# Four 1024-column additions on GpSimd become eight of 512 columns, each placed behind a VectorE split; the FFN sums get a buffer of their own

## The chip, the core and the metric

The kernel runs on one core of one Trainium2 chip. The metric is the device time of one execution in microseconds (us). A profiled execution leaves a trace: for every engine each instruction with its start and its duration. TensorE (PE) multiplies matrices, VectorE (DVE), ScalarE (ACT) and GpSimd (POOL) work element by element, SyncE (SP) issues transfers. The engines run apart from one another and meet at semaphores: an instruction waits until a counter has reached a value, and adds to one when it is done.

## What is computed

The input x has 2 x 2048 tokens of 256 values. After a layer norm, two branches work on the normed value xn, and both are added to x.

```
xn = layernorm(x)
h  = xn + cosformer_attn(rmsnorm(xn, norm1_w), qkv_w, qkv_b, out_w, out_b)
m  = gelu(rmsnorm(h, norm2_w) @ mlp_w1 + mlp_b1) @ mlp_w2 + mlp_b2
f  = relu(xn @ ternary(w_fc).T + gate * low_rank(xn)) ** 2 @ ternary(w_proj).T
out = x + (h + m) + f
```

The attention is causal and linear: q and k go through a relu, are weighted with cosines and sines of the position, and each token sums over those before it.

## The kernel before

Eight tiles (t = 0 to 7) of 512 tokens, 256 of each batch, pass one after the other through a body that is written once per engine. In a body PE goes through these stages: four chunks of attention (j = 0 to 3; scores, the context within and across chunks, and the update of a running `state`), between them the first blocks of the FFN branch, then the output projection, the rest of the FFN, and last eight MLP blocks (m = 0 to 7). In the MLP stage PE takes `mlp_up(m)` and then `mlp_down(m - 1)`; between them it also makes k, q, z and v of the next tile. The order on each engine is that of its code; there is no scheduler.

Matrix products are made in float32 of reduced width, so each operand that matters is held as a high and a low part. The low part of a hidden block comes from VectorE: `split(n)` (L945) subtracts `wide_hi` from `wide`, n = 0 to 7 for the FFN blocks, n = 8 to 15 for the MLP blocks. It waits for ScalarE, which writes `wide` and then `wide_hi` (`hi_done`), and PE's `down(n)` (L1194) waits for it (`lo_done`). Thus each `mlp_down(m)` needs `split(8 + m)`.

GpSimd has four additions of 128 partitions x 1024 columns in a tile, each over all four blocks of 128 tokens:

- L496: `xn` plus the row `ob_row`, right after `trig_q(0)` (L484, two products of 256 columns that weight q of chunk 0; each chunk has such a pair);
- L524: `res = xb + ctxn`, behind `split(7)`; `ctxn` holds h by then, `xb` holds x plus the MLP's second bias;
- L530: `res = res + ctxn`, where VectorE has meanwhile overwritten `ctxn` with the scaled FFN sums (L1033); it waits for `split(9)` and for the split of the next tile's q (`q_parts_done`, the last L795);
- L465: `x_plus_b2`, which refills `xb` for the next tile.

L1033 waits for L524, since both use `ctxn`. At the end VectorE adds the MLP sums to `res` (L1053) and SP sends it out. GpSimd also adds to `state` once per chunk (L510), after VectorE's masked product `mask_update` (L975). `layernorm` (L769) on VectorE makes the next `xn` behind `split(12)`. SP spreads k and q of the next tile by 12 and 24 transfers (`k_stack`, `q_stack`); `trig_q(0)` of that tile waits for the last of them.

Of the kernel before, what the change touches and what calls it, by code (L numbers as in the profile page):

```python
# [84 lines left out]
def program(nc, x, qkv_w, qkv_b, out_w, out_b, norm1_w, norm2_w, mlp_w1, mlp_b1, mlp_w2, mlp_b2,  # L85
            fast_b, w_fc, w_proj, u, v, gate, consts, trig, out):
    with ExitStack() as ctx:
# [268 lines left out]
        @block.sync  # L356
        def _(sp):
            def load_x(t):
                for b in range(B):
                    sp.dma_start(xin[:, 2 * b:2 * b + 2, :],  # L360
                                 x[b, bass.ds(t * POS, POS), :].rearrange("(c p) e -> p c e", p=P)).then_inc(x_in, 16)

            def load_tab(t):
                sp.dma_start(tab[:, :], trig[bass.ds(t, 1), :, :].rearrange("a p n -> p (a n)")).then_inc(tab_in, 16)

            load_x(0)
            sp.dma_start(n1w[:, :], norm1_w.rearrange("(k p) -> p k", p=P),
                         allow_slow_non_contiguous=True).then_inc(in_n1, 16)
            sp.dma_start(raw_qkv, qkv_w.rearrange("(k p) n -> p k n", p=P)).then_inc(in_qkv, 16)
            sp.dma_start(cst[:, :], consts).then_inc(in_const, 16)  # L370
            sp.dma_start(v_raw, v).then_inc(in_fb, 16)
            sp.dma_start(fbT, fast_b.rearrange("r k -> k r"), allow_slow_non_contiguous=True).then_inc(in_fb, 16)
            sp.dma_start(raw_fc, w_fc.rearrange("(m p) n -> p m n", p=P)).then_inc(in_fc, 16)
            sp.dma_start(raw_wo, out_w.rearrange("(k p) n -> p k n", p=P)).then_inc(in_wo, 16)
            smalls = [
                (qkb[:, :], qkv_b[0:2 * E].rearrange("(k p) -> p k", p=P)),
                (n2w[:, :], norm2_w.rearrange("(k p) -> p k", p=P)),
                (u_raw, u.rearrange("(m p) r -> p m r", p=P)),
                (gate_col[:, :], gate.broadcast_to([P, 1])),
                (vb_row[:, :], qkv_b[2 * E:3 * E].rearrange("(a n) -> a n", a=1).broadcast_to([P, E])),  # L380
                (b2_row[:, :], mlp_b2.rearrange("(a n) -> a n", a=1).broadcast_to([P, E])),
                (ob_row[:, :], out_b.rearrange("(a n) -> a n", a=1).broadcast_to([P, E])),
                (b1[:, :], mlp_b1.rearrange("(k p) -> p k", p=P)),
            ]
            assert len(smalls) == N_SMALL
            for dst, src in smalls:
                sp.dma_start(dst, src, allow_slow_non_contiguous=True).then_inc(in_small, 16)
            sp.dma_start(raw_pr, w_proj.rearrange("(m p) n -> p m n", p=P)).then_inc(in_pr, 16)
            load_tab(0)

            sp.wait_ge(shared_full, KE)
            sp.dma_start(raw_w1[0], mlp_w1[0:P, :]).then_inc(in_w1[0], 16)

            def stack(t):

                sp.wait_ge(k_parts_done, (t + 1) * 2 * KE)
                if not isinstance(t, int) or t:
                    sp.wait_ge(shared_full, shared_use(t - 1, S_SCORE + 4 * NB))
                for g in range(4):
                    for slot, part in enumerate((0, 0, 1)):  # L400
                        sp.dma_start(k_stack[slot:P:4, g, :, :].bitcast(F32),
                                     k_parts[32 * g:32 * g + 32, part, :, :]).then_inc(k_stacked, 16)
                sp.wait_ge(q_parts_done, (t + 1) * 2 * KE)
                for g in range(4):
                    stack_q(sp, g, 1, 1, q_lo_stacked)
                for g in range(2 if isinstance(t, int) and t == 0 else 4):
                    for slot in (0, 2):
                        stack_q(sp, g, slot, 0, q_hi_stacked[g // 2])

            sp.wait_ge(stack_zero, 3)  # L410
            stack(0)

            def body(t, more):
                if more:

                    sp.wait_ge(xn_done, (t + 1) * NB)
                    sp.wait_ge(xb_done, t + 1)
                    sp.wait_ge(xs_done, (t + 1) * NB)
                    load_x(t + 1)

                    sp.wait_ge(q_trig_done, (t + 1) * 2 * NB)
                    sp.wait_ge(v_trig_done, (t + 1) * 2 * NB)
                    load_tab(t + 1)
                    stack(t + 1)
                for b in range(B):
                    sp.wait_ge(out_done, t * 2 + b + 1)
                    sp.dma_start(out[b, bass.ds(t * POS, POS), :].rearrange("(c p) e -> p c e", p=P),
                                 res[:, 2 * b:2 * b + 2, :]).then_inc(out_sent, 16)

            body(0, True)  # L430
            with sp.Fori(1, NT - 1) as t:
                body(t, True)
            body(NT - 1, False)
            sp.wait_ge(out_sent, NT * 32)


        @block.gpsimd
        def _(pool):
# [21 lines left out]
                pool.wait_ge(ln_pow, t * N_POW + POW_MSQ)  # L460
                pool.tensor_tensor(msq_eps[:, :], msq[:, :], rms_eps[:, :], ALU.add).then_inc(ln_pow, 1)

            def x_plus_b2(t):

                pool.tensor_tensor(xb[:, :, :], xin[:, :, :],  # L465
                                   b2_row[:, :].rearrange("p (a n) -> p a n", a=1).broadcast_to([P, NB, E]),
                                   ALU.add).then_inc(xb_done, 1)

            pool.memset(q_stack[:, 0:2, :, :, :].rearrange("p g r m n -> p (g r m n)").bitcast(F32),
                        0.0).then_inc(stack_zero, 1)  # L470
# [4 lines left out]
            def body(t, more):  # L475
# [14 lines left out]
                for i in range(2):  # L490
                    pool.wait_ge(q_hi_stacked[i], (t + 1) * N_Q_HI * 16)
                trig_q(0)

                pool.wait_ge(xs_done, (t + 1) * NB)
                pool.wait_ge(xn_done, (t + 1) * NB)
                pool.tensor_tensor(xn[:, :, :], xn[:, :, :],  # L496
                                   ob_row[:, :].rearrange("p (a n) -> p a n", a=1).broadcast_to([P, NB, E]),
                                   ALU.add).then_inc(xnb_done, 1)

                for j in range(NB):  # L500
                    if j + 1 < NB:
                        trig_q(j + 1)
                    if isinstance(t, int) and t == 0 and j == 0:
                        pool.wait_ge(in_small, 16 * N_SMALL)
                        pool.wait_ge(w1_lo_done, KE)
                        x_plus_b2(0)
                    pool.wait_ge(upd_free, t * N_UPD + 2 + j)
                    pool.wait_ge(across_done, t * NB + j + 1)
                    later(pool, upd_used, t * NB + max(j - 1, 0))
                    pool.tensor_tensor(state[:, j % B, :, :], state[:, j % B, :, :], added[:, :, :],  # L510
                                       ALU.add).then_inc(upd_used, 1)
# [3 lines left out]
                for g in range(2):  # L515
# [2 lines left out]
                    pool.tensor_tensor(ms2[:, two], mean_sq[:, two], rms_eps[:, two], ALU.add).then_inc(r2_done, 1)  # L518
                    pool.wait_ge(r2_done, t * 4 + 2 * g + 1)
                    pool.tensor_tensor(r2[:, two], ms2[:, two], half[:, two], ALU.pow).then_inc(r2_done, 1)  # L520
                pool.wait_ge(shared_free, shared_use(t, S_OUT + 1) + 1)
                pool.wait_ge(lo_done, t * 2 * HB + HB)
                later(pool, out_sent, t * 32)
                pool.tensor_tensor(res, xb[:, :, :], ctxn, ALU.add).then_inc(res_done, 1)  # L524
                pool.wait_ge(ffn_done, (t + 1) * NB)
                pool.wait_ge(lo_done, t * 2 * HB + HB + 2)
                if more:
                    pool.wait_ge(q_parts_done, (t + 2) * 2 * KE)
                pool.wait_ge(res_done, t * 2 + 1)
                pool.tensor_tensor(res, res, ctxn, ALU.add).then_inc(res_done, 1)  # L530
                if more:
                    keep_msq(t + 1)
                    pool.wait_ge(x_in, t * 32 + 64)
                    x_plus_b2(t + 1)

            body(0, True)
            with pool.Fori(1, NT - 1) as t:
# [199 lines left out]
        def _(dve):  # L737
# [203 lines left out]
            def body(t, more):  # L941
# [16 lines left out]
                def context(j):  # L958
# [2 lines left out]
                    dve.reciprocal(recip[:, :], heads[:, :, D]).then_inc(recip_done, 1)  # L961
                    dve.wait_ge(recip_done, t * NB + j + 1)
                    if j == 0:
                        later(dve, res_done, t * 2)
                    dve.tensor_tensor(ctxn[:, chunk_block(j), :].rearrange("p (h e) -> p h e", e=D), heads[:, :, 0:D],
                                      recip[:, :].rearrange("p (h a) -> p h a", a=1).broadcast_to([P, H, D]),
                                      ALU.mult).then_inc(ctx_free, 1)
# [43 lines left out]
                                      ALU.subtract).then_inc(shared_free, 1)  # L1011
                split(5)

                dve.wait_ge(xnb_done, t + 1)
                for g in range(2):
                    dve.wait_ge(shared_full, shared_use(t, S_OUT + g) + 1)
                    dve.tensor_tensor(ctxn[:, 2 * g:2 * g + 2, :].rearrange("p b n -> p (b n)"), shared[g][:, :],
# [10 lines left out]
                                      ALU.subtract).then_inc(shared_free, 1)  # L1028

                dve.wait_ge(wide_used, t * 2 * HB + HB)  # L1030
                dve.wait_ge(res_done, t * 2 + 1)
                for k in range(NB):
                    dve.scalar_tensor_tensor(ctxn[:, k, :], accum[k // 2][:, (k % 2) * E:(k % 2 + 1) * E],  # L1033
                                             msq_eps[:, k:k + 1], pr_scale_row[:, :],
                                             ALU.mult, ALU.mult).then_inc(ffn_done, 1)
                if more:
# [10 lines left out]
                    z_lo(t + 1)  # L1047
                    v_rows(t + 1, 0)

                dve.wait_ge(res_done, t * 2 + 2)  # L1050
                dve.wait_ge(wide_used, (t + 1) * 2 * HB)
                for g in range(2):
                    dve.tensor_tensor(res[:, 2 * g:2 * g + 2, :].rearrange("p b n -> p (b n)"), accum[g][:, :],  # L1053
# [364 lines left out]
```

## Time and profile before

| | |
|---|---|
| time, median of 3 runs | 640.94 us (640.76 to 641.73) |
| the profiled execution's own time | 644.8 us |
| its span, first to last instruction | 641.9 us |
| mean granted clock of PE | 0.988 |
| PE busy | 589.1 us (92%) |
| VectorE busy | 421.8 us (66%) |
| ScalarE busy | 367.5 us (57%) |
| GpSimd busy | 217.9 us (34%) |

Of the profiled execution's time 2.9 us lie outside its span. It took 3.9 us more than the median of the runs that were only timed. A busy share is an average over stages with different limits: which wait ends last must be read from the stage.

### The profile page before, as it was taken

What the parts mean: (1) busy time and instruction counts of PE and PEld (TensorE: products, weight loads), DVE (VectorE), ACT (ScalarE), POOL (GpSimd) and SP (SyncE); (2) the same over time, 40 slices, a digit from 0 to 9 for tenths busy, and PEclk for the clock granted to TensorE, in tenths of its full rate; (3) what the DMA queues carried; (4) which work ended last, traced back from release to release, by engine and by line L of the source; (5) the groups of instructions that cost most, each with busy time, mean ns of one, the idle gap of its engine ahead of it and who ended that gap; (6) DMA issues with size and microseconds to landing.
All of it is one profiled execution on the core that took longest, in us unless ns stands there. A gap on an engine that the chain in (4) does not pass through costs nothing.

```text
span 641.9 us, 14501 instructions
## 1 busy us (share of the span) xinstructions
PE 589.1 (92%) x5070; PEld 515.2 (80%) x5070; DVE 421.8 (66%) x776; ACT 367.5 (57%) x654; POOL 217.9 (34%) x219
## 2 busy tenths in 40 slices
PE   2757999989999999999999999999999999999986
PEld 2646878978888888888889887888879888888876
DVE  7689966477655766477664876558674786647542
ACT  5465583546745566465845657455754658455643
POOL 6006333153233432153432432334420533333220
PEclk9969999989999999999999999999999999999999
DMA  7771005600065002620056000740036200540000
GB/s 205 213 188 49 17 1 128 137 2 19 1 150 113 16 0 66 121 74 16 0 122 113 26 16 14 148 100 16 0 90 106 65 16 0 135 94 2 2 1 33
DMA packets 27992, 42.01 MB, mean 65 GB/s; under 512 B 9008, under 2 KB 19904, under 8 KB 27968
## 3 DMA queue, kind: packets, MB, share of 16 engines
q1 hardware_dynamic: 26528, 39.59, 26.7%
q10 hardware_dynamic: 1440, 2.10, 1.2%
q8 instruction: 15, 0.25, 0.2%
q14 instruction: 9, 0.07, 0.0%
HBM read 12.31 MB, written 4.19 MB: 26 GB/s over the span
## 4 chain that ended last, share of the span: by engine, by line
PE 78%; DVE 8%; ACT 6%; issue 2%; SPq 2%; ACTq 1%; DMA 1%; POOL 0%; DVEq 0%
PE accum L1194 20%; PE dense L1179 8%; PE dense L1356 8%; PE shared L1217 5%; DVE wide_lo L945 5%; PE ctx_ps L1242 5%; PE dense L1229 4%; PE dense L1090 4%; PE dense L1361 4%; PE shared L1330 4%; PE shared L1104 3%; PE ctx_ps L1253 2%; PE dense L1094 2%; PE dense L1184 2%; PE upd_ps L1267 2%
## 5 line engine op out<-in xcount | busy, mean ns | idle before, releaser
L945 DVE TENSOR_TENSOR wide_lo<-wide,wide_hi 128x512 fp32r<-128x512 f32 x128 | 116.7, 913 | 81.3 <-ACT wide_hi L672 74.4
L484 POOL TENSOR_TENSOR arena<-arena,tab 128x256 f32<-128x256 f32 x64 | 50.1, 804 | 142.3 <-DMA q_stack<-arena 142.3
L953 DVE TENSOR_TENSOR weighted<-shared,cst 128x512 f32<-128x512 f32 x128 | 82.8, 683 | 18.1 <-PE shared L1217 17.9
L669 ACT ACTIVATE wide<-dense,b 128x512 f32<-128x512 f32 x64 | 44.1, 690 | 80.6 <-PE dense L1361 80.2
L510 POOL TENSOR_TENSOR state<-state,added 128x544 f32<-128x544 f32 x32 | 43.6, 1363 | 115.5 <-DVE added L975 115.5
L1194 PE MATMUL accum<-w_hi,wide_hi 128*128 128x256 f32 x256 | 73.5, 287 | 8.0 <-DVE wide_lo L945 8.0
L1194 PE MATMUL accum<-prT,wide_hi 128*128 128x256 f32 x256 | 66.7, 287 | 6.8 <-DVE wide_lo L945 6.8
L1194 PE MATMUL accum<-w_lo,wide_hi 128*128 128x256 f32 x256 | 71.9, 281 | 0.0
L1194 PE MATMUL accum<-w_hi,wide_lo 128*128 128x256 f32 x256 | 71.8, 280 | 0.0
L659 ACT ACTIVATE wide<-dense,scales 128x512 f32<-128x512 f32 x64 | 44.1, 689 | 43.4 <-PE dense L1184 35.4
L1194 PE MATMUL accum<-prT,wide_lo 128*128 128x256 f32 x256 | 65.2, 281 | 0.0
L699 ACT ACTIVATE ctxT<-dense,cst 128x512 f32<-128x512 f32 x32 | 22.1, 689 | 68.6 <-PE dense L1229 68.6
L1194 PEld LDWEIGHTS accum<-w_hi,wide_hi 128*128 128x128 f32 x256 | 48.1, 188 | 15.7 <-DVE wide_lo L945 12.3
L1356 PE MATMUL dense<-cT_hi,w_hi 128*128 128x512 f32 x128 | 52.3, 409 | 6.7 <-ACT cT_hi L718 6.7
L1194 PEld LDWEIGHTS accum<-prT,wide_hi 128*128 128x128 f32 x256 | 48.3, 189 | 9.5 <-DVE wide_lo L945 5.2
L1179 PE MATMUL dense<-xT_hi,fcT 128*128 128x512 f32 x128 | 52.1, 407 | 0.8 <-ACT prT L625 0.8
L1217 PE MATMUL shared<-q_stack,k_stack 128*128 128x256 f32 x256 | 51.8, 304 | 0.7 <-DVE weighted L953 0.7
L1179 PE MATMUL dense<-xT_lo,fcT 128*128 128x512 f32 x128 | 50.8, 397 | 0.0
L1356 PE MATMUL dense<-cT_hi,w_lo 128*128 128x512 f32 x128 | 50.6, 395 | 0.0
L1194 PEld LDWEIGHTS accum<-w_lo,wide_hi 128*128 128x128 f32 x256 | 48.1, 188 | 1.7
L1194 PEld LDWEIGHTS accum<-prT,wide_lo 128*128 128x128 f32 x256 | 48.3, 189 | 1.0
L1194 PEld LDWEIGHTS accum<-w_hi,wide_lo 128*128 128x128 f32 x256 | 48.4, 189 | 0.0
(166 smaller groups left out, 1438.5 us busy)
## 6 DMA issues: line engine op xcount, KB each, us to landing
k_stack<-weighted SPq DMA_DIRECT2D x96, 128.0 KB, 2.7
q_stack<-arena SPq DMA_DIRECT2D x184, 64.0 KB, 2.3
xin<-L_attn_x SPq DMA_DIRECT2D x16, 256.0 KB, 2.9
out<-late SPq DMA_DIRECT2D x16, 256.0 KB, 2.3
tab<-trig SPq DMA_DIRECT2D x8, 258.0 KB, 2.7
arena<-L_ffn_w_fc SPq DMA_DIRECT2D x1, 1024.0 KB, 8.5
late<-L_ffn_w_proj SPq DMA_DIRECT2D x1, 1024.0 KB, 7.0
late<-L_attn_mlp_w ACTq DMA_DIRECT2D x1, 1024.0 KB, 5.5
```

Of the source, the lines that this page charges most:

```text
L484: pool.tensor_tensor(q_trig[:, j % 2, r, :, :], qT[:, :, k * P:(k + 1) * P], row.broadcast_to([P, KE, P]), ALU.mult).then_inc(q_trig_done, 1)
L510: pool.tensor_tensor(state[:, j % B, :, :], state[:, j % B, :, :], added[:, :, :], ALU.add).then_inc(upd_used, 1)
L659: act.activation(wide[:, m % 2, :], dense[ffn_place(m) % 2][:, :], ACT.Relu, scale=scales[:, m:m + 1]).then_inc(dense_free, 1)
L669: act.activation(wide[:, m % 2, :], dense[m % 2][:, :], ACT.Gelu_apprx_tanh, bias=b1[:, m:m + 1]).then_inc(dense_free, 1)
L945: dve.tensor_tensor(wide_lo[:, n % 2, :], wide[:, n % 2, :], wide_hi[:, n % 2, :].bitcast(F32), ALU.subtract).then_inc(lo_done, 1)
L953: dve.tensor_tensor(weighted[:, g, :].rearrange("p (a n) -> p a n", a=4), shared[g % 2][:, :].rearrange("p (a n) -> p a n", a=4), mask.rea ...
L1090: pe.matmul(bank[:, :], w[:, k, cols], xT_hi[:, k, :], start=(k == 0 and c == 0), stop=False)
L1179: pe.matmul(bank[:, :], fcT[:, i // 2, cols], (xT_hi, xT_lo)[i % 2][:, i // 2, :], start=(i == 0), stop=False)
L1194: mm = pe.matmul(accum[k // 2][:, (k % 2) * E:(k % 2 + 1) * E], a[:, n % 2, tok], w[:, n % HB, :], start=(first and i == 0 and k % 2 == 0) ...
L1217: mm = pe.matmul(bank[:, i * 2 * P:(i + 1) * 2 * P].rearrange("p (r n) -> p r n", r=2), k_stack[:, row, m, tok], q_stack[:, row, :, m, tok ...
L1242: mm = pe.matmul(heads[:, m * (H // KE):(m + 1) * (H // KE), 0:VW], q_trig[:, j % 2, r, m, :], state[:, j % B, m, r * HW:(r + 1) * HW].rea ...
L1356: pe.matmul(bank[:, :], w[:, k, cols], cT_hi[:, k, :], start=(k == 0 and i == 0), stop=False)
```

## The change

The additions work on two blocks of tokens (512 columns) at a time. Their places on GpSimd are set by `behind_split(m)`, which waits until `split(8 + m)` is done, and, for `xn`, by a wait for `split(j + 1)` of the attention chunk. The scaled FFN sums go to `res` and no longer to `ctxn`; `xb` takes x + bias + h, and `res` then adds `xb`. VectorE's L1033 waits for the last output to be sent (`out_sent`) in place of L524.

```diff
-                    sp.wait_ge(xb_done, t + 1)
+                    sp.wait_ge(xb_done, (t + 1) * 4)
...
-            def x_plus_b2(t):
-                pool.tensor_tensor(xb[:, :, :], xin[:, :, :],
-                                   b2_row[:, :].rearrange("p (a n) -> p a n", a=1).broadcast_to([P, NB, E]),
-                                   ALU.add).then_inc(xb_done, 1)
+            def x_plus_b2(t, g):
+                two = slice(2 * g, 2 * g + 2)
+                pool.tensor_tensor(xb[:, two, :], xin[:, two, :],
+                                   b2_row[:, :].rearrange("p (a n) -> p a n", a=1).broadcast_to([P, 2, E]),
+                                   ALU.add).then_inc(xb_done, 2)
...
                 trig_q(0)
-                pool.wait_ge(xs_done, (t + 1) * NB)
-                pool.wait_ge(xn_done, (t + 1) * NB)
-                pool.tensor_tensor(xn[:, :, :], xn[:, :, :],
-                                   ob_row[:, :].rearrange("p (a n) -> p a n", a=1).broadcast_to([P, NB, E]),
-                                   ALU.add).then_inc(xnb_done, 1)
+                def xn_plus_ob(j):
+                    pool.wait_ge(xn_done, (t + 1) * NB)
+                    pool.wait_ge(lo_done, t * 2 * HB + j + 2)
+                    two = slice(2 * j - 2, 2 * j)
+                    pool.tensor_tensor(xn[:, two, :], xn[:, two, :],
+                                       ob_row[:, :].rearrange("p (a n) -> p a n", a=1).broadcast_to([P, 2, E]),
+                                       ALU.add).then_inc(xnb_done, 1)
                 for j in range(NB):
                     if j + 1 < NB:
                         trig_q(j + 1)
                     if isinstance(t, int) and t == 0 and j == 0:
...
-                        x_plus_b2(0)
+                        for g in range(2):
+                            x_plus_b2(0, g)
+                    if 1 <= j <= 2:
+                        xn_plus_ob(j)
...
+                def behind_split(m):
+                    pool.wait_ge(lo_done, t * 2 * HB + HB + m + 1)
                 pool.wait_ge(shared_free, shared_use(t, S_OUT + 1) + 1)
-                pool.wait_ge(lo_done, t * 2 * HB + HB)
-                later(pool, out_sent, t * 32)
-                pool.tensor_tensor(res, xb[:, :, :], ctxn, ALU.add).then_inc(res_done, 1)
-                pool.wait_ge(ffn_done, (t + 1) * NB)
-                pool.wait_ge(lo_done, t * 2 * HB + HB + 2)
                 if more:
                     pool.wait_ge(q_parts_done, (t + 2) * 2 * KE)
-                pool.wait_ge(res_done, t * 2 + 1)
-                pool.tensor_tensor(res, res, ctxn, ALU.add).then_inc(res_done, 1)
+                for g in range(2):
+                    two = slice(2 * g, 2 * g + 2)
+                    behind_split(1 + g)
+                    pool.tensor_tensor(xb[:, two, :], xb[:, two, :], ctxn[:, two, :], ALU.add).then_inc(res_done, 1)
+                for g in range(2):
+                    two = slice(2 * g, 2 * g + 2)
+                    behind_split(3 + g)
+                    pool.wait_ge(ffn_done, t * NB + 2 * g + 2)
+                    pool.wait_ge(res_done, t * 4 + g + 1)
+                    pool.tensor_tensor(res[:, two, :], res[:, two, :], xb[:, two, :], ALU.add).then_inc(res_done, 1)
                 if more:
                     keep_msq(t + 1)
                     pool.wait_ge(x_in, t * 32 + 64)
-                    x_plus_b2(t + 1)
+                    for g in range(2):
+                        behind_split(5 + g)
+                        pool.wait_ge(res_done, t * 4 + 3 + g)
+                        x_plus_b2(t + 1, g)
...
                 dve.wait_ge(wide_used, t * 2 * HB + HB)
-                dve.wait_ge(res_done, t * 2 + 1)
+                later(dve, out_sent, t * 32)
                 for k in range(NB):
-                    dve.scalar_tensor_tensor(ctxn[:, k, :], accum[k // 2][:, (k % 2) * E:(k % 2 + 1) * E],
+                    dve.scalar_tensor_tensor(res[:, k, :], accum[k // 2][:, (k % 2) * E:(k % 2 + 1) * E],
```

The other lines of the diff only fit the counts of `res_done` and `xnb_done`.

The order of instructions changes on GpSimd alone. Here is the start of a tile there, in the looped body, before the change; `arena<-arena,tab` is `trig_q`, `state` the running sums.

```order
L484 TENSOR_TENSOR arena<-arena,tab 128x256 x2
L494 REGISTER_ALU
L496 TENSOR_TENSOR xn<-xn,ob_row 128x1024
L484 TENSOR_TENSOR arena<-arena,tab 128x256 x2
L507 ISA
L508 REGISTER_ALU
L510 TENSOR_TENSOR state<-state,added 128x544
```

With the change the same place reads as follows.

```order
L485 TENSOR_TENSOR arena<-arena,tab 128x256 x4
L514 ISA
L515 REGISTER_ALU
L517 TENSOR_TENSOR state<-state,added 128x544
L485 TENSOR_TENSOR arena<-arena,tab 128x256 x2
L497 REGISTER_ALU
L498 ISA
L500 TENSOR_TENSOR xn<-xn,ob_row 128x512
L514 REGISTER_ALU
L515 REGISTER_ALU
L517 TENSOR_TENSOR state<-state,added 128x544
```

`trig_q(1)` follows `trig_q(0)` at once, and the two halves of the `xn` addition stand ahead of the `state` additions of chunks 1 and 2.

The end of the body on GpSimd, the MLP stage, before the change (`late` holds `res` and `ctxn`):

```order
L524 TENSOR_TENSOR late<-xb,late 128x1024
L526 REGISTER_ALU
L528 ISA
L529 REGISTER_ALU
L530 TENSOR_TENSOR late<-late 128x1024
L460 REGISTER_ALU
L461 TENSOR_TENSOR msq_eps<-msq,rms_eps 128x4
L533 REGISTER_ALU
L465 TENSOR_TENSOR xb<-xin,b_row 128x1024
```

And with the change:

```order
L537 TENSOR_TENSOR xb<-xb,late 128x512
L529 REGISTER_ALU
L537 TENSOR_TENSOR xb<-xb,late 128x512
L529 REGISTER_ALU
L543 TENSOR_TENSOR late<-late,xb 128x512
L529 REGISTER_ALU
L543 TENSOR_TENSOR late<-late,xb 128x512
L460 REGISTER_ALU
L461 TENSOR_TENSOR msq_eps<-msq,rms_eps 128x4
L546 ISA
L529 REGISTER_ALU
L466 TENSOR_TENSOR xb<-xin,b_row 128x512
```

Three additions became six; they wait for `split(9)` to `split(14)` in turn, and the first also for `q_parts_done`, which only the second did before.

## Rows read from the trace of the kernel before

**Rows 1.** Who waited for whom: us in total, times, longest.
```profile
PE accum L1194 <- DVE wide_lo L945: 14.7, 17, 2.4
```

**Rows 2.** Groups by line and shape, GpSimd: count, busy us, mean ns, idle before.
```profile
L510 POOL TENSOR_TENSOR state<-state,added 128x544 f32<-128x544 f32 x32 | 43.6, 1363 | 115.5 <-DVE added L975 115.5
...
L530 POOL TENSOR_TENSOR late<-late 128x1024 f32<-128x1024 f32 x8 | 19.1, 2391 | 84.5 <-DVE arena L795 81.0 <-DVE wide_lo L945 3.6
```

**Rows 3.** The same view, VectorE.
```profile
L945 DVE TENSOR_TENSOR wide_lo<-wide,wide_hi 128x512 fp32r<-128x512 f32 x128 | 116.7, 913 | 81.3 <-ACT wide_hi L672 74.4 <-ACT wide_hi L664 6.8
```

**Rows 4.** Timeline, GpSimd, end of tile 3 and start of tile 4: start, duration.
```profile
328.85 2.39 POOL L530 TENSOR_TENSOR late<-late 128x1024 f32<-128x1024 f32 x1 [11.41 <-DVE arena L795]
...
331.80 2.41 POOL L465 TENSOR_TENSOR xb<-xin,b_row 128x1024 f32<-128x1024 f32 x1
349.39 1.44 POOL L484 TENSOR_TENSOR arena<-arena,tab 128x256 f32<-128x256 f32 x2 [15.19 <-DMA q_stack<-arena]
350.79 2.40 POOL L496 TENSOR_TENSOR xn<-xn,ob_row 128x1024 f32<-128x1024 f32 x1
353.15 1.87 POOL L484 TENSOR_TENSOR arena<-arena,tab 128x256 f32<-128x256 f32 x2
...
364.74 1.37 POOL L510 TENSOR_TENSOR state<-state,added 128x544 f32<-128x544 f32 x1 [3.13 <-DVE added L975]
...
370.61 1.37 POOL L510 TENSOR_TENSOR state<-state,added 128x544 f32<-128x544 f32 x1 [3.11 <-DVE added L975]
```

**Rows 5.** Timeline, VectorE, the same stretch.
```profile
328.00 0.69 DVE L795 TENSOR_TENSOR arena<-arena 128x512 fp32r<-128x512 f32 x1
329.67 2.11 DVE L945 TENSOR_TENSOR wide_lo<-wide,wide_hi 128x512 fp32r<-128x512 f32 x1 [0.98 <-ACT wide_hi L672]
332.49 2.27 DVE L945 TENSOR_TENSOR wide_lo<-wide,wide_hi 128x512 fp32r<-128x512 f32 x1 [0.71 <-ACT wide_hi L672]
336.43 0.69 DVE L945 TENSOR_TENSOR wide_lo<-wide,wide_hi 128x512 fp32r<-128x512 f32 x1 [1.67 <-ACT wide_hi L672]
337.04 1.38 DVE L769 TENSOR_SCALAR xn<-xin,mean,rstd 128x256 f32<-128x256 f32 x4
...
353.15 1.28 DVE L945 TENSOR_TENSOR wide_lo<-wide,wide_hi 128x512 fp32r<-128x512 f32 x1
...
362.39 0.68 DVE L945 TENSOR_TENSOR wide_lo<-wide,wide_hi 128x512 fp32r<-128x512 f32 x1
```

**Rows 6.** Timeline, PE, the same stretch: first products of a `down`.
```profile
328.00 0.28 PE L1194 MATMUL accum<-w_hi,wide_hi 128*128 128x256 f32 x1
...
331.84 0.39 PE L1194 MATMUL accum<-w_hi,wide_hi 128*128 128x256 f32 x1 [0.85 <-DVE wide_lo L945]
...
340.55 0.28 PE L1194 MATMUL accum<-w_hi,wide_hi 128*128 128x256 f32 x1
...
343.36 0.28 PE L1194 MATMUL accum<-w_hi,wide_hi 128*128 128x256 f32 x1
...
354.49 0.39 PE L1194 MATMUL accum<-prT,wide_hi 128*128 128x256 f32 x1 [0.44 <-DVE wide_lo L945]
...
358.64 0.75 PE L1217 MATMUL shared<-q_stack,k_stack 128*128 128x256 f32 x4
```

**Rows 7.** Timeline, SP's queue, the same stretch: the q transfers.
```profile
332.17 15.16 SPq L350 DMA_DIRECT2D q_stack<-arena  x24
```

**Rows 8.** Timeline, start of tile 1, PE.
```profile
130.02 0.38 PE L1194 MATMUL accum<-prT,wide_hi 128*128 128x256 f32 x1 [1.81 <-DVE wide_lo L945]
...
135.76 0.73 PE L1217 MATMUL shared<-q_stack,k_stack 128*128 128x256 f32 x4
```

**Rows 9.** Windows: stretch, length, busy of PE, PEld, DVE, ACT, POOL, PEclk, DMA.
```profile
132.00:134.00 2.00, 2.00 (x9) 1.69 (x7) 0.46 (x1) 0.00 (x0) 0.00 (x0) 0.50 0.00 0
```

**Rows 10.** Timeline, PE, start of tile 0.
```profile
51.39 0.36 PE L1194 MATMUL accum<-prT,wide_hi 128*128 128x256 f32 x1 [2.44 <-DVE wide_lo L945]
```

**Rows 11.** Timeline, PE, MLP stage of the last tile.
```profile
616.76 0.36 PE L1194 MATMUL accum<-w_hi,wide_hi 128*128 128x256 f32 x1 [1.17 <-DVE wide_lo L945]
```

More of the change, by code:

```diff
@@ L963, in context @@
                     if j == 0:
-                        later(dve, res_done, t * 2)
+                        later(dve, res_done, t * 4)
                     dve.tensor_tensor(ctxn[:, chunk_block(j), :].rearrange("p (h e) -> p h e", e=D), heads[:, :, 0:D],
@@ L1012, in body @@
                 split(5)
-                dve.wait_ge(xnb_done, t + 1)
+                dve.wait_ge(xnb_done, 2 * (t + 1))
                 for g in range(2):
@@ L1048, in body @@
                     v_rows(t + 1, 0)
-                dve.wait_ge(res_done, t * 2 + 2)
+                dve.wait_ge(res_done, (t + 1) * 4)
                 dve.wait_ge(wide_used, (t + 1) * 2 * HB)
```

## The prediction

> **What bounds the kernel now.** I read the page's table first: PE is busy almost throughout, so only what makes PE wait can cost time. The list of waits says what that is: the `down` products on PE waited for VectorE's `split` 17 times, 14.7 us in all [rows 1]. The other engines wait far longer, but for PE. So the question is why `split` is late.
>
> The groups by line show `split` with a mean of 913 ns [rows 3], while an undisturbed one takes 0.69 us [rows 5]. The timelines of GpSimd and VectorE, laid side by side, show which ones are long: the `split` that starts at 329.67 while L530 runs, the one at 332.49 while L465 runs, and the one at 353.15 while a `trig_q` product runs [rows 4, 5]. In each case it ends about 0.54 us after the GpSimd instruction: 329.67 + 2.11 = 331.78 against 328.85 + 2.39 = 331.24. So a VectorE subtraction with both inputs in SBUF stands still while a GpSimd product or sum runs, and then does its work.
>
> The Trainium skill states this as a rule ("SBUF — State Buffer", section "SBUF: two separate sides"): the two engines share a pair of ports, and who starts first holds it for the whole instruction. The trace agrees, with the 0.54 us above.
>
> On PE the wait for the `split` of 329.67 is seen at 331.84 as 0.85 us of idling [rows 6]. The whole loss is more, since the next product restarts slowly and the next `split` is late too. The undisturbed period of the MLP stage is 343.36 - 340.55 = 2.81 us. From 328.00 to 340.55 lie four periods, 11.24 us, but it took 12.55: 1.31 us lost per tile [rows 6]. It happens in tiles 0 to 6, where L530 waits for the next tile's q.
>
> **The change, part by part.** The work on GpSimd stays the same but for eight more starts; GpSimd has long idle times, so only where a piece lies counts. The trace of before has no piece of 512 columns. Its neighbours are 544 columns at 1363 ns and 1024 at 2391 ns [rows 2]; a line through both gives 1.29 us, and bounds are 1.2 and 1.36.
>
> *MLP stage.* The first piece (`xb` + h) can start where L530 started, at 328.85, since the q split ends there. It ends at 328.85 + 1.29 = 330.14. The `split` of 329.67 still collides with it, and ends 0.54 later, at 330.68. PE is ready for it at 328.00 + 2.81 = 330.81, so it no longer waits, with 0.13 us to spare. The second piece starts behind that `split`, some 0.16 us after it, as L530 did behind the q split (328.69 to 328.85) [rows 4, 5], and lasts from 330.84 to 332.13. The next `split` was released at 332.49, so it is free. Pieces 3 to 6 follow their `split` in the same way: 0.69 + 0.16 + 1.29 = 2.14 us of a period of 2.81. Only behind `split(12)` is there other work, `layernorm` with 1.38 us [rows 5], see the rivals. So nearly all of the 1.31 us comes back; bounds are 0.55 (rival 1) and 1.31, and I take 1.2, because one margin is only 0.13. Seven tiles: **8.4 us**.
>
> *Start of tiles 2 to 7.* L496 moves away, and `trig_q(1)` follows `trig_q(0)`. Four products of 1.44 / 2 = 0.72 us run from 349.39, when the q transfers have landed, to 352.27 [rows 4]. `split(0)` would be due at 353.15 - 1.3 = 351.85, because PE arrives earlier by the gain of the MLP stage. It is blocked by the last product until 352.27 and ends at 352.81. PE, which idled 0.44 us until 354.49, would be ready at 354.05 - 1.3 = 352.75 [rows 6]. Left over is about 0.1 of 0.44 us; bounds 0 and 0.44, I take 0.35. Six tiles: **2.1 us**.
>
> *Start of tile 1.* Here L496 itself held `split(0)`, and PE idled 1.81 us. From its restart to the scores of chunk 1 PE took 135.76 - 130.02 = 5.74 us, where tile 4 took 358.64 - 354.49 = 4.15 [rows 6, 8]. The extra 1.59 us lie in a stretch whose granted clock is 0.50, the lower of the two levels, 1.2 GHz [rows 9]. It follows the longest idle time of PE since the tile loop got going. With `trig_q(1)` in L496's place I leave 0.15 of the 1.81 us. Whether the clock then stays up is open: bounds 0 and 1.59, I take 1.2, since nothing else sets this tile apart. Together **2.85 us**.
>
> *Start of tile 0.* PE idled 2.44 us [rows 10], in the same way. Here the two halves of `x_plus_b2` still run at once behind `trig_q(1)` and will hold back the subtraction that splits the MLP's second weights, as L465 does now. Bounds: 1.0, if what is won at `split(0)` is largely lost there, and 4.0, if all of it is gone; I take **2.0 us**, nearer to the lower one, since VectorE has more work there than PE.
>
> *The FFN sums in `res`.* L1033 waits for L524 no more. In tiles 0 to 6 this is worth nothing: PE has q and k of the next tile to make before it needs the sums. In the last tile it has not, and idles 1.17 us [rows 11]; ScalarE's and VectorE's blocks ahead of that product remain, so of 0 to 1.17 I take **0.4 us**. The wait that replaces it, for the last tile's output, has been met for most of a tile.
>
> *The halves of the `xn` sum ahead of `state`.* The first waits for `split(2)`, which ends at 362.39 + 0.68 = 363.07, so it lies between 363.23 and 364.52. The `state` sum behind it started at 364.74 [rows 4, 5]: nothing is late. Next to it VectorE only has work that reads PSUM or one SBUF input. Cost 0. If the half came later than that, see rival 3.
>
> *Later waits.* `xb` is refilled some 9 us later than now; SP asks for it only behind the output of the tile. Cost 0.
>
> Sum: 8.4 + 2.1 + 2.85 + 2.0 + 0.4 = 15.75 us. Against the profiled execution's own 644.8 this gives 629.05. The runs without a profile had a median of 640.94, 3.9 us less; I carry the same gain over: 640.94 - 15.75 = **625.2 us**.
>
> **Rivals.**
>
> *1. The pieces collide anew (634.4 us).* Behind `split(12)` VectorE's `layernorm` of 1.38 us and piece 4 of 1.29 us may exclude one another. Then `split(13)` comes 1.38 + 1.29 = 2.67 us after `split(12)`, against a period of 2.81, and its own 0.69 no longer fits: PE waits some 0.5 us. If the first piece also starts 0.3 us later than L530, its margin of 0.13 is gone. Of 1.31 us then 0.55 remain, 3.9 us in seven tiles; the tile starts give nothing but 1.65 in tile 1 and 1.0 in tile 0: 6.5 us. For it speaks the narrow margin; against it, that PE takes `mlp_down(5)` about half a period, 1.4 us, after its `split` was due. The skill speaks for it: the section "Who interferes with whom" of "SBUF — State Buffer" names tensor_scalar, which `layernorm` is, among the contenders. No row here shows the two at once.
>
> *2. The gain is only moved (640.9 us).* A faster PE could run into the q transfers. SP issues them from 332.17 for 15.16 us [rows 7], and they have landed when `trig_q(0)` starts at 349.39. That chain hangs on when k and q were split, ahead of the stall that goes. So the tile's length would not change if PE waited for it already. But `split(0)`, which stands behind the tile's first scores on VectorE, started 3.8 us later, at 353.15 [rows 4, 5], and the MLP's 1.3 us do not use that up.
>
> *3. Slower (645.7 us).* The `state` sums stand behind the halves of `xn`. If a half is late, `state` is late, then VectorE's next `mask_update`, which waits for it, and PE's next update. The sum of 364.74 ends at 366.1; the next one starts at 370.61 [rows 4], and the mask just ahead of it, so an estimated 3.5 us are free. A half as long as L496 still leaves 2.5. It decides only from a lateness of 3.5 us on, in two chunks of eight tiles; with the gain used up and 0.3 us more in each of 16, 4.8 us, it is 640.9 + 4.8.
>
> **How the numbers follow.** Chances: my forecast 0.74, rival 1 0.17, rival 2 0.04, rival 3 0.05. A measurement of this kernel can tell about 0.2%, 1.3 us, from no change; so faster 0.91, same 0.04, slower 0.05. All bounds at their best give 7 x 1.31 + 6 x 0.44 + 3.4 + 4.0 + 1.17 = 20.4, or 620.5 us. Upwards the range reaches towards rival 1 without holding all of it: 620.5 to 633.
>
> **What would show it.** Right: the mean of `split` falls from 913 to below 780 ns; PE's waits for it fall from 14.7 to about 3 us; MLP periods between 328 and 343 all read 2.81; the period of a tile in the loop falls by 1.6 us; no stretch at the lower clock at tile 1. Wrong: a long `split(13)` or `layernorm` beside the fourth piece, `split(0)` as late as now behind `trig_q(1)`, or PE waiting for `q_stack` at a tile's start. The forecast fails most likely if pieces last much longer than 1.29 us.

## The result and the profile after

The changed kernel takes 626.1 us (median of four runs, 625.3 to 626.23), the kernel before beside it 641.34. The ratio is 0.975, 95% interval 0.9731 to 0.9769. The prediction was 625.2 us, range 620.5 to 633.

PE's list of waits shows where the time came from (us in total, times, longest). It answers to [rows 1]:

```profile
PE accum L1210 <- DVE wide_lo L961: 2.4, 3, 0.9
```

14.7 us of waiting for `split` became 2.4. The three waits that are left are 0.79 us at tile 0 and 0.86 and 0.75 us in the last tile. The groups by line on VectorE (`split` is L961 now, `layernorm` L785) say the same of the cause: the mean of `split` fell from 913 ns [rows 3] to 712, which is close to the undisturbed 0.69 us.

```profile
L961 DVE TENSOR_TENSOR wide_lo<-wide,wide_hi 128x512 fp32r<-128x512 f32 x128 | 91.0, 712 | 86.4 <-ACT wide_hi L688 78.6 <-ACT wide_hi L680 7.2
```

The halves on GpSimd, in the same view, take 1.28 to 1.34 us in the mean (the longest of the four lines is shown); 1.29 had been worked out from the neighbours in [rows 2].

```profile
L543 POOL TENSOR_TENSOR late<-late,xb 128x512 f32<-128x512 f32 x16 | 21.4, 1339 | 22.2 <-DVE wide_lo L961 22.2
```

The timeline of GpSimd from the end of tile 3 to the start of tile 4, the stretch of [rows 4]:

```profile
318.20 1.29 POOL L537 TENSOR_TENSOR xb<-xb,late 128x512 f32<-128x512 f32 x1 [16.17 <-DVE arena L811]
320.12 1.30 POOL L537 TENSOR_TENSOR xb<-xb,late 128x512 f32<-128x512 f32 x1 [0.63 <-DVE wide_lo L961]
...
325.46 1.40 POOL L543 TENSOR_TENSOR late<-late,xb 128x512 f32<-128x512 f32 x1 [1.55 <-DVE wide_lo L961]
...
331.15 1.29 POOL L466 TENSOR_TENSOR xb<-xin,b_row 128x512 f32<-128x512 f32 x1 [1.48 <-DVE wide_lo L961]
338.66 2.81 POOL L485 TENSOR_TENSOR arena<-arena,tab 128x256 f32<-128x256 f32 x4 [6.22 <-DMA q_stack<-arena]
```

And VectorE in the same stretch, beside [rows 5]:

```profile
319.03 1.02 DVE L961 TENSOR_TENSOR wide_lo<-wide,wide_hi 128x512 fp32r<-128x512 f32 x1 [0.98 <-ACT wide_hi L688]
...
324.69 0.69 DVE L961 TENSOR_TENSOR wide_lo<-wide,wide_hi 128x512 fp32r<-128x512 f32 x1 [2.15 <-ACT wide_hi L688]
325.30 2.35 DVE L785 TENSOR_SCALAR xn<-xin,mean,rstd 128x256 f32<-128x256 f32 x4
327.57 0.68 DVE L961 TENSOR_TENSOR wide_lo<-wide,wide_hi 128x512 fp32r<-128x512 f32 x1
...
341.29 0.74 DVE L961 TENSOR_TENSOR wide_lo<-wide,wide_hi 128x512 fp32r<-128x512 f32 x1
```

The first half starts when the split of the next tile's q is done, and each of the others behind a `split`. Only the first one still holds a `split` back: 1.02 us, ending at 320.05, 0.56 behind the half's end at 319.49. The fourth half lies beside `layernorm`, which takes 2.35 us in place of 1.38; `split(13)` follows at once and is just not late. On PE (first products of `down(1)`, `down(2)`, `down(5)` and `down(6)`, of the first FFN `down` of tile 4 with the two products ahead of it, and the scores of its chunk 1, as in [rows 6]) no row has an idle time before it:

```profile
317.36 0.28 PE L1210 MATMUL accum<-w_hi,wide_hi 128*128 128x256 f32 x1
...
320.18 0.30 PE L1210 MATMUL accum<-w_hi,wide_hi 128*128 128x256 f32 x1
...
328.66 0.28 PE L1210 MATMUL accum<-w_hi,wide_hi 128*128 128x256 f32 x1
...
331.48 0.28 PE L1210 MATMUL accum<-w_hi,wide_hi 128*128 128x256 f32 x1
...
341.79 0.39 PE L1233 MATMUL shared<-q_stack,k_stack 128*128 128x256 f32 x2
342.08 0.38 PE L1210 MATMUL accum<-prT,wide_hi 128*128 128x256 f32 x1
...
346.23 0.73 PE L1233 MATMUL shared<-q_stack,k_stack 128*128 128x256 f32 x4
```

Four MLP periods take 328.66 - 317.36 = 11.30 us; they took 12.55, so 1.25 us came back per tile. From `down(6)` to the scores of chunk 1 it is 346.23 - 331.48 = 14.75 us; it was 358.64 - 343.36 = 15.28: 0.53 us per tile start.

In the first two tiles and in the last one PE's rows read (answering to [rows 8, 10, 11]):

```profile
49.73 0.36 PE L1210 MATMUL accum<-prT,wide_hi 128*128 128x256 f32 x1 [0.79 <-DVE wide_lo L961]
...
124.58 0.39 PE L1210 MATMUL accum<-prT,wide_hi 128*128 128x256 f32 x1
...
128.73 0.74 PE L1233 MATMUL shared<-q_stack,k_stack 128*128 128x256 f32 x4
...
598.85 0.36 PE L1210 MATMUL accum<-w_hi,wide_hi 128*128 128x256 f32 x1 [0.86 <-DVE wide_lo L961]
```

### The profile page after: what moved, and what is told of

It is laid out like the page before. It is cut to its first block, busy times and chain, and to the rows that moved or that the text cites. A ratio compares the mean times of both kernels' runs of the same rounds, so it can differ in the third digit from the quotient of the medians.

```text
span 624.0 us, 14580 instructions
## 1 busy us (share of the span) xinstructions
PE 584.1 (94%) x5070; PEld 514.5 (82%) x5070; DVE 402.4 (64%) x776; ACT 367.5 (59%) x654; POOL 220.2 (35%) x251
## 4 chain that ended last, share of the span: by engine, by line
PE 85%; ACT 5%; DVE 4%; SPq 2%; issue 1%; ACTq 1%; DMA 1%; DVEq 0%
PE accum L1210 22%; PE dense L1372 9%; PE dense L1195 9%; PE shared L1233 6%; PE ctx_ps L1258 5%; PE dense L1377 5%; PE dense L1245 4%; PE dense L1106 4%; PE shared L1346 4%; PE shared L1120 3%; PE ctx_ps L1269 2%; PE dense L1200 2%; PE dense L1110 2%; PE upd_ps L1283 2%; PE shared L1326 1%
## 5 line engine op out<-in xcount | busy, mean ns | idle before, releaser
L961 DVE TENSOR_TENSOR wide_lo<-wide,wide_hi 128x512 fp32r<-128x512 f32 x128 | 91.0, 712 | 86.4 <-ACT wide_hi L688 78.6
L485 POOL TENSOR_TENSOR arena<-arena,tab 128x256 f32<-128x256 f32 x64 | 48.1, 778 | 78.5 <-DMA q_stack<-arena 78.5
L1210 PE MATMUL accum<-w_hi,wide_hi 128*128 128x256 f32 x256 | 72.2, 282 | 1.6 <-DVE wide_lo L961 1.6
L537 POOL TENSOR_TENSOR xb<-xb,late 128x512 f32<-128x512 f32 x16 | 20.7, 1294 | 129.2 <-DVE arena L811 114.0
```

The source lines that it names most:

```text
L485: pool.tensor_tensor(q_trig[:, j % 2, r, :, :], qT[:, :, k * P:(k + 1) * P], row.broadcast_to([P, KE, P]), ALU.mult).then_inc(q_trig_done, 1)
L961: dve.tensor_tensor(wide_lo[:, n % 2, :], wide[:, n % 2, :], wide_hi[:, n % 2, :].bitcast(F32), ALU.subtract).then_inc(lo_done, 1)
L1210: mm = pe.matmul(accum[k // 2][:, (k % 2) * E:(k % 2 + 1) * E], a[:, n % 2, tok], w[:, n % HB, :], start=(first and i == 0 and k % 2 == 0) ...
```

## The experiments

The theory: a `split`, both of whose inputs lie in SBUF, stands still while a GpSimd addition or product runs; only where this carries its end past the moment at which PE needs it does it cost time. So the place of an addition decides, and its size only through the place. Rivals: the halving itself is what helps, since VectorE gets in between two halves; or the freed buffer is, since VectorE no longer waits for GpSimd before L1033.

**The `xn` addition put back** (the changed kernel, one edit):

```diff
                 trig_q(0)
...
+                pool.wait_ge(xn_done, (t + 1) * NB)
+                pool.tensor_tensor(xn[:, :, :], xn[:, :, :],
+                                   ob_row[:, :].rearrange("p (a n) -> p a n", a=1).broadcast_to([P, NB, E]),
+                                   ALU.add).then_inc(xnb_done, 2)
...
-                    if 1 <= j <= 2:
-                        xn_plus_ob(j)
```

> The changed kernel, but the addition of ob_row to xn is again one piece of 1024 columns right behind trig_q(0). Theory (the place of an addition against the splits decides): split(0) of every tile stands still again, PE idles at each tile's start as before; against the changed kernel's 626.1 us it loses about 0.52 us in each of six tiles, 1.9 in tile 1 and about 1.7 in tile 0, 6.7 us, and 1.6 more if the lower clock at tile 1 comes back: 633 to 635 us. Rival (only the MLP stage counts): 626 to 628 us.

Measured: 635.91 us, 0.9911 of the kernel before (0.9887 to 0.9936), a gain of 6.4 us. The start of tile 4 in its timelines, GpSimd, VectorE and PE:

```profile
345.74 2.40 POOL L496 TENSOR_TENSOR xn<-xn,ob_row 128x1024 f32<-128x1024 f32 x1
```
```profile
346.97 1.71 DVE L955 TENSOR_TENSOR wide_lo<-wide,wide_hi 128x512 fp32r<-128x512 f32 x1
```
```profile
348.74 0.39 PE L1204 MATMUL accum<-prT,wide_hi 128*128 128x256 f32 x1 [0.87 <-DVE wide_lo L955]
```

More was lost than the stalls of before, and than the expected 633 to 635 us allow: at tile 4 PE idles 0.87 us, where it idled 0.44 [rows 6]. The MLP stage gives PE 1.25 us, so `split(0)` is due earlier, but `trig_q(0)` and the addition behind it start when the q transfers land, which has not moved. The `split` now falls into the 1024-column addition itself, which it had narrowly missed.

**The `xn` addition alone moved** (the kernel before, with `xn_plus_ob(j)` as in the change, and nothing else of it).

> The kernel before, with nothing changed but the xn addition, which stands in two halves behind split(2) and split(3). Theory: the seven MLP stalls of 1.23 us stay, and tile 0 keeps its whole x_plus_b2; the rest of the gain comes: about 626.1 + 8.6 + 0.5 = 635 us. The gains of this and of the run with xn put back add up to about the whole gain of 15 us. Rival (parts help only together, or only the MLP counts): 640 us or more.

Measured: 636.11 us, 0.9903 (0.9883 to 0.9924), a gain of 6.2 us. The two parts give 6.4 + 6.2 = 12.6 us, together they gave 15.2. By the three intervals the difference of 2.6 us is good to some 2.4 us, an estimate. Most of it can be found in what the run above lost too much. In tiles 3 to 7 of its profile PE idles 0.80 to 0.97 us at the tile's start, in place of 0.37 to 0.44 in the profile of the kernel before: 2.3 us more in the five tiles. Tile 1 idles less, 0.31 us in place of 1.81, and tile 2 more, 1.94 in place of 0.50, so these two nearly cancel:

```profile
127.26 0.38 PE L1204 MATMUL accum<-prT,wide_hi 128*128 128x256 f32 x1 [0.31 <-DVE wide_lo L955]
...
201.79 0.39 PE L1204 MATMUL accum<-prT,wide_hi 128*128 128x256 f32 x1 [1.94 <-DVE wide_lo L955]
```

Both parts count, and the gains do not add up: the moved additions of the MLP stage give all they have only when the `xn` addition is moved too. That they would add up was a miss.

**Whole additions behind splits** (the changed kernel; the MLP stage's halves joined again):

```diff
-                for g in range(2):
-                    two = slice(2 * g, 2 * g + 2)
-                    behind_split(1 + g)
-                    pool.tensor_tensor(xb[:, two, :], xb[:, two, :], ctxn[:, two, :], ALU.add).then_inc(res_done, 1)
...
+                behind_split(2)
+                pool.tensor_tensor(xb[:, :, :], xb[:, :, :], ctxn, ALU.add).then_inc(res_done, 2)
+                behind_split(3)
...
+                pool.tensor_tensor(res, res, xb[:, :, :], ALU.add).then_inc(res_done, 2)
...
+                    behind_split(5)
...
+                    pool.tensor_tensor(xb[:, :, :], xin[:, :, :], for_all, ALU.add).then_inc(xb_done, 4)
```

> The changed kernel, but the MLP stage's additions are three whole pieces of 1024 columns, behind split(10), split(11) and split(13). Theory of place: a piece of 2.39 us runs past the next split's release by about 0.4 us and holds it back by about 1 us, which PE's reserve of half a period, 1.4 us, covers: 626 to 628 us, though split's mean rises. Rival (the halving is what helps): the stalls of 1.3 us per tile return, about 634 us.

Measured: 628.69 us, 0.9785 (0.9766 to 0.9804). Of some 8.7 us that the MLP stage gave, all but about 2 stay without any halving. VectorE and PE, tile 3's MLP stage (on PE the first products of `down(1)`, `down(3)`, `down(4)` and `down(6)`):

```profile
324.13 0.96 DVE L957 TENSOR_TENSOR wide_lo<-wide,wide_hi 128x512 fp32r<-128x512 f32 x1 [2.13 <-ACT wide_hi L684]
326.96 1.22 DVE L957 TENSOR_TENSOR wide_lo<-wide,wide_hi 128x512 fp32r<-128x512 f32 x1 [1.86 <-ACT wide_hi L684]
```
```profile
319.64 0.28 PE L1206 MATMUL accum<-w_hi,wide_hi 128*128 128x256 f32 x1
...
325.29 0.28 PE L1206 MATMUL accum<-w_hi,wide_hi 128*128 128x256 f32 x1
...
328.23 0.39 PE L1206 MATMUL accum<-w_hi,wide_hi 128*128 128x256 f32 x1
...
333.98 0.28 PE L1206 MATMUL accum<-w_hi,wide_hi 128*128 128x256 f32 x1
```

The first `split` ends at 325.09, before PE's 325.29; the second at 328.18, after PE would have been ready at 325.29 + 2.81 = 328.10. So the reserve is not the 1.4 us of the expectation. A `split` that is released at 326.96 may take until 328.10, 1.14 us; 0.69 of them it needs for itself, and 0.45 are free. The places were right, the size of the reserve was not, and the expected 626 to 628 us was missed by 0.7.

**Halves without places** (the changed kernel; `behind_split` stands only ahead of the first of the six halves).

> The changed kernel, but the six half additions of the MLP stage wait for no split of their own: they start when the next tile's q is split and follow one another. Theory of place: each split that falls into them is held back by up to 1.3 + 0.54 us less than a whole piece would; PE's reserve of 1.4 us is overrun by about 0.5 us once or twice per tile: 629 to 633 us. Rival (the size alone does it, VectorE gets in between two pieces): 626 us.

Measured: 629.88 us, 0.9809 (0.9789 to 0.9829), inside the expected 629 to 633 us. The timelines of GpSimd, VectorE and PE (`down(1)` and `down(6)`):

```profile
320.45 2.99 POOL L537 TENSOR_TENSOR xb<-xb,late 128x512 f32<-128x512 f32 x2 [16.19 <-DVE arena L809]
323.41 2.98 POOL L542 TENSOR_TENSOR late<-late,xb 128x512 f32<-128x512 f32 x2
```
```profile
321.28 1.02 DVE L959 TENSOR_TENSOR wide_lo<-wide,wide_hi 128x512 fp32r<-128x512 f32 x1 [0.98 <-ACT wide_hi L686]
324.09 1.15 DVE L959 TENSOR_TENSOR wide_lo<-wide,wide_hi 128x512 fp32r<-128x512 f32 x1 [1.80 <-ACT wide_hi L686]
326.94 1.40 DVE L959 TENSOR_TENSOR wide_lo<-wide,wide_hi 128x512 fp32r<-128x512 f32 x1 [1.69 <-ACT wide_hi L686]
```
```profile
319.61 0.28 PE L1208 MATMUL accum<-w_hi,wide_hi 128*128 128x256 f32 x1
...
334.19 0.28 PE L1208 MATMUL accum<-w_hi,wide_hi 128*128 128x256 f32 x1
```

VectorE does get in between two halves, and GpSimd then waits for it: two halves take 2.99 us, not 2.6. So halving alone takes most of the stall away too, since a `split` waits for the rest of 1.3 us and not of 2.4. From `down(1)` to `down(6)` PE took 343.36 - 328.00 = 15.36 us before [rows 6], just as long with the `xn` addition alone moved, and takes 331.48 - 317.36 = 14.12 with the change. With whole additions in their places it is 333.98 - 319.64 = 14.34, with halves without places 334.19 - 319.61 = 14.58. Of the 1.24 us, place alone brings 1.02 and halving alone 0.78. So the theory's last sentence was too strong: size also helps without the place. The times of the two runs alone hardly tell them apart, since their intervals overlap. With both, place and size, nothing is late.

**The buffer alone** (the kernel before):

```diff
-                later(pool, out_sent, t * 32)
-                pool.tensor_tensor(res, xb[:, :, :], ctxn, ALU.add).then_inc(res_done, 1)
+                pool.tensor_tensor(xb[:, :, :], xb[:, :, :], ctxn, ALU.add).then_inc(res_done, 1)
...
-                pool.tensor_tensor(res, res, ctxn, ALU.add).then_inc(res_done, 1)
+                pool.tensor_tensor(res, res, xb[:, :, :], ALU.add).then_inc(res_done, 1)
...
+                    pool.wait_ge(res_done, t * 2 + 2)
...
-                dve.wait_ge(res_done, t * 2 + 1)
+                later(dve, out_sent, t * 32)
                 for k in range(NB):
-                    dve.scalar_tensor_tensor(ctxn[:, k, :], ...
+                    dve.scalar_tensor_tensor(res[:, k, :], ...
```

> The kernel before, with nothing changed but the buffers: GpSimd adds h into xb, VectorE writes the scaled FFN sums to res without waiting for GpSimd, and GpSimd adds xb to res; sizes and places stay. Theory: the wait that goes was off PE's path but for the last tile: 0 to 0.5 us faster, no change that can be told. Rival (the freed VectorE makes its splits early): several us faster, 635 us or less.

Measured: 641.67 us, 1.0005 (0.9993 to 1.0017). No change can be told in the time. The profile shows an effect in the last tile, where PE idles 0.86 us in place of 1.17 [rows 11], 0.31 us less:

```profile
613.61 0.36 PE L1194 MATMUL accum<-w_hi,wide_hi 128*128 128x256 f32 x1 [0.86 <-DVE wide_lo L945]
```

**The `xn` addition whole, but behind `split(2)`** (the changed kernel, one piece of 1024 columns in chunk 1 in place of two halves).

> The changed kernel, but the xn addition is one piece of 1024 columns behind split(2), ahead of the state addition of chunk 1. Theory: the state addition of chunk 1 starts about 0.8 us late, inside a reserve of some 3.5 us, and no split falls into the piece: 626.1 us within 0.2%. Rival (the state additions behind it are near PE's path): 16 chunk delays become one longer one per tile, slower by 3 us or more.

Measured: 627.02 us, 0.9773 (0.9759 to 0.9786), against 0.9767 for the changed kernel in the same series. GpSimd, chunk 1 of tile 4:

```profile
351.93 2.38 POOL L499 TENSOR_TENSOR xn<-xn,ob_row 128x1024 f32<-128x1024 f32 x1 [1.61 <-DVE wide_lo L960]
354.27 1.37 POOL L516 TENSOR_TENSOR state<-state,added 128x544 f32<-128x544 f32 x1
```

The `state` addition starts some 0.8 us later than it could: VectorE's `mask_update` ended at 353.21, and in chunk 0 the `state` addition started 0.23 us behind it. It ends at 355.64, and VectorE's next `mask_update` starts at 358.36. No cost of the late addition, and no gain of halving `xn`, can be told.

**Two more places** (the changed kernel; `trig_q(1)` behind `split(0)`, and tile 0's `x_plus_b2` behind `split(1)`):

```diff
                 for j in range(NB):
+                    if j == 0:
+                        pool.wait_ge(lo_done, t * 2 * HB + 1)
                     if j + 1 < NB:
                         trig_q(j + 1)
...
                         pool.wait_ge(w1_lo_done, KE)
+                        pool.wait_ge(lo_done, 2)
                         for g in range(2):
```

> The changed kernel, and trig_q(1) of each tile also waits for split(0), and tile 0's two halves of x_plus_b2 wait for split(1). Theory: in tile 0 the split, the cast and the subtraction that stood still by 0.41, 0.58 and 0.95 us go free, 1.0 to 1.9 us; in tiles 1 to 7 at most 0.1 us each; 624.3 to 625.3 us. Rival (trig_q(1) or the state addition comes too late for PE): 626 us or more.

Measured: 623.8 us, 0.9721 (0.9707 to 0.9734). The changed kernel as it is, in the same series:

> The changed kernel as it is, for the comparison on the same chip: 626 us, 0.975 of the kernel before.

Measured: 626.86 us, 0.9767 (0.9754 to 0.9781). The added places give about 3 us more, the lowest time measured here, and more than the 624.3 to 625.3 us expected. VectorE at the start of tile 0, with the added places:

```profile
48.38 0.69 DVE L964 TENSOR_TENSOR wide_lo<-wide,wide_hi 128x512 fp32r<-128x512 f32 x1 [0.21 <-ACT wide_hi L683]
...
50.19 0.68 DVE L850 CAST w_hi<-late 128x512 fp32r<-128x512 f32 x1
50.91 0.69 DVE L852 TENSOR_TENSOR w_lo<-late,w_hi 128x512 fp32r<-128x512 f32 x1
```

And in the first profile of the changed kernel (the last row is the next cast of the same shape):

```profile
48.49 1.10 DVE L961 TENSOR_TENSOR wide_lo<-wide,wide_hi 128x512 fp32r<-128x512 f32 x1 [0.36 <-ACT wide_hi L680]
...
50.71 1.01 DVE L847 CAST w_hi<-late 128x512 fp32r<-128x512 f32 x1
51.75 1.64 DVE L849 TENSOR_TENSOR w_lo<-late,w_hi 128x512 fp32r<-128x512 f32 x1
...
53.92 0.41 DVE L847 CAST w_hi<-late 128x512 fp32r<-128x512 f32 x1
```

The three together are 1.7 us shorter on VectorE. PE shows what that is worth: its scores of chunk 2 of tile 0 start at 55.15 with the added places and at 56.98 in the profile of the same series without them, 1.83 us apart:

```profile
56.98 0.51 PE L1233 MATMUL shared<-q_stack,k_stack 128*128 128x256 f32 x2 [0.68 <-DVE weighted L969]
```
```profile
55.15 0.50 PE L1236 MATMUL shared<-q_stack,k_stack 128*128 128x256 f32 x2
```

At the start of tile 2 the distance grows by 0.56 us, since `split(0)` there took 1.24 us beside `trig_q(1)` and takes 0.68 now that `trig_q(1)` waits for it. The other 0.6 us come in steps of about 0.1 and less in the later tiles.

**The kernel before, profiled twice more**, for the lower clock at tile 1.

> The kernel before as it is, one more profile. If the lower clock at tile 1 belongs to PE's idle time there, the stretch behind the first down of tile 1 shows a granted clock near 0.5 again and takes about 5.7 us up to the next scores; if it comes and goes, it takes 4.15 us at 1.00, and the profiled execution is 1.6 us shorter than the first one.

> The same once more: with the profile of the first runs, three samples of where the lower clock lies.

Measured: 643.7 and 640.33 us. The start of tile 1 on PE, in the first and in the second:

```profile
130.79 0.39 PE L1194 MATMUL accum<-prT,wide_hi 128*128 128x256 f32 x1 [1.69 <-DVE wide_lo L945]
...
134.94 0.74 PE L1217 MATMUL shared<-q_stack,k_stack 128*128 128x256 f32 x4
```
```profile
127.89 0.39 PE L1194 MATMUL accum<-prT,wide_hi 128*128 128x256 f32 x1 [0.19 <-DVE wide_lo L945]
...
132.05 0.75 PE L1217 MATMUL shared<-q_stack,k_stack 128*128 128x256 f32 x4
```

They take 4.15 and 4.16 us to the next scores, at the full clock. The idle time itself changes, 1.81, 1.69 and 0.19 us. It hangs on when the q transfers have landed, so that `trig_q(0)` and the addition behind it can start: 2.11 us ahead of PE's first scores of the tile in the last execution (123.48 against 125.59), 0.55 ahead in the one before (126.44 against 126.99) and 0.43 in the first (125.66 against 126.09). The last run had the lower clock in another place, at tile 0 (a window of 2 us, PEclk is the third figure from the end):

```profile
51.00 0.55 PE L1194 MATMUL accum<-prT,wide_hi 128*128 128x256 f32 x1 [2.43 <-DVE wide_lo L945]
```
```profile
52.00:54.00 2.00, 2.00 (x9) 1.90 (x9) 1.97 (x3) 0.00 (x0) 2.00 (x2) 0.50 0.00 0
```

## Why the prediction was right

*The cause.* Right: the splits that a GpSimd instruction overlapped were PE's waits, and moving those instructions took 12.3 of 14.7 us of waiting away.

*MLP stage*, 8.4 us forecast: 7 x 1.25 = 8.75. The first half still holds a `split` back and PE is just not late, as worked out; the whole additions showed how small the reserve is, 0.45 us. The forecast's own rows give it too: an undisturbed `split` of 329.67 would have ended at 330.36, and PE would have been ready at 330.81.

*Starts of tiles 2 to 7*, 2.1 us: 6 x 0.53 = 3.2. Too small by about 0.18 us per tile. Half of that is the 0.1 us of idling that I left to `trig_q(1)`'s last product: that product did not make PE wait at tile 4. The other half was not counted: without an idle time PE's next product starts 0.10 us ahead of the recorded end of the one before it (342.08 against 341.79 + 0.39), so an idle time of 0.44 us costs 0.53.

*Tile 0*, 2.0 us: 2.44 - 0.79 = 1.65 at the first `down`, and some 0.5 at a later wait.

*Last tile and buffer*, 0.4 us: 1.17 - 0.86 = 0.31, with the buffer alone as with the whole change; in the time of the run with the buffer alone this could not be told from no change.

*Tile 1*, 2.85 us, is the term that was mis-sized. In the first profile it gave 1.81 + 1.59 = 3.4 us, since the lower clock was gone after the change. But of three profiled executions of the kernel before only the first had the 1.59 us of lower clock there, and the idle time of 1.81 was 0.19 in another. Without the lower clock the tile is worth between 0.2 and 1.8 us. I had read a mechanism of the kernel from one sample of it.

Together the first profile and the one after differ by 17.9 us of span, more than the 15.75 of the sum; the timed medians differ by 15.2. The first profiled execution took 3.9 us more than the median that its gain was carried over to. With the other terms as measured, 8.75 + 3.2 + 2.15 + 0.31 = 14.4 us, and 0.2 to 1.8 us for tile 1, the sum is 14.6 to 16.2 us, around the 15.2. The 2.1 us for the starts of tiles 2 to 7 were too small, and the 2.85 us for tile 1 too large for an execution without the lower clock. So the nearness of 625.2 to 626.1 is in part luck, while range and direction rest on the shown mechanism.

*Rival 1* was half right in mechanism: `layernorm` and the fourth half do hold one another up (2.35 us in place of 1.38), which the prediction had listed as a sign of being wrong. It costs nothing, because `split(13)` starts at 327.57, 2.19 us behind the end of `split(12)` and not 2.67, and ends at 328.25, 0.41 us before PE's 328.66. The argument against the rival, a reserve of 1.4 us, was wrong; 0.45 is what there is. The Trainium skill's rule that it leaned on ("SBUF — State Buffer", section "Who interferes with whom") holds here, with those 2.35 us, and with the cast of 1.01 us at tile 0 that takes 0.41 undisturbed. *Rivals 2 and 3* did not come; a `state` addition that was 0.8 us late cost nothing that can be told, and the lateness of 3.5 us at which rival 3 begins was not run. One slip: the change adds four starts on GpSimd per tile, not eight.

## What to carry to other kernels

Lay the timelines of VectorE and GpSimd side by side and compare one VectorE instruction where GpSimd is idle with the same where it runs. If it stands still, put GpSimd's work behind the VectorE instruction that PE waits for, so that it ends before the next one is released. In the MLP stage place gave more than size (1.02 against 0.78 of 1.24 us), and either alone gave most of it. When work is moved to gain time, look again at what else was just missing a collision, since other starts, here those set by transfers, do not move along.

## What the runs showed of the hardware

The lower clock of PE did not follow the length of the idle time: with 2.44 us of idling at tile 0 the clock stayed at 1.00 in one execution of the kernel before and fell to 0.50 in another with 2.43; at tile 1 it fell once after 1.81 us and not after 1.69. Over all runs, PE idled 1.69 us or more at a tile's start nine times, and the clock fell in three of them; in the seven profiles in which no tile's start idled 1 us it did not fall at one. What decides it stays open. GpSimd is held up by VectorE as well: two halves with a `split` between them took 2.99 us and not 2.6.
